# Cross-attention on one core: another order of GpSimd's last instructions, one sum moved to VectorE, and a mixing product placed ahead of four transposes

## The reference

```
text_p  = H_l @ W_text + b_text            # H_l = x: (4, 2048, 512)
audio_p = H_a @ W_audio + b_audio          # H_a: (4, 77, 384)
Q = layer_norm(text_p, g1, beta1);  K = layer_norm(audio_p, g2, beta2);  V = audio_p
alpha = softmax(Q @ K^T / sqrt(512))       # (4, 2048, 77)
out = layer_norm(alpha @ V @ W_out + b_out + H_l, g_out, beta_out)
```

## Time and profile before

| what | value |
|---|---|
| median of three runs | 271.36 us |
| the profiled execution, its own time | 270.91 us |
| span of the profile | 269.2 us |
| granted TensorE clock, mean | 0.994 |
| TensorE matmul, busy | 253.6 us (94%) |
| VectorE, busy | 234.1 us (87%) |
| ScalarE, busy | 207.2 us (77%) |
| GpSimd, busy | 207.4 us (77%) |
| moved by DMA | 43.25 MB |

### The profile page before, as it was taken

The page is one execution under the profiler, slowest core; times in us unless marked ns, Lnnn a source line. Parts: engine busy times, 40 slices in busy tenths (PEclk is TensorE's granted clock), DMA queues, the critical chain, the costliest instruction groups (busy, mean ns, idle before and its releaser), DMA issues.

```text
span 269.2 us, 5946 instructions
## 1 busy us (share of the span) xinstructions
PE 253.6 (94%) x1667; PEld 232.3 (86%) x1667; DVE 234.1 (87%) x719; ACT 207.2 (77%) x516; POOL 207.4 (77%) x232
## 2 busy tenths in 40 slices
PE   7799999999999999999999999999999999999750
PEld 6578878989999989999999999999999999999520
DVE  3867489978999998999999999999999999998594
ACT  3766348235788888989988898888889889999681
POOL 6057440011189999999999999999999999999985
PEclk9999999999999999999999999999999999999997
DMA  6926099532225553544555445444444455442217
GB/s 195 266 80 195 2 280 393 151 131 72 78 80 168 167 175 138 175 160 157 177 181 179 168 169 173 165 156 156 156 158 159 169 169 162 160 171 108 106 46 273
DMA packets 19456, 43.25 MB, mean 161 GB/s; under 512 B 2050, under 2 KB 2382, under 8 KB 19434
## 3 DMA queue, kind: packets, MB, share of 16 engines
q1 hardware_dynamic: 18810, 41.96, 46.6%
q10 hardware_dynamic: 624, 1.06, 1.4%
HBM read 21.19 MB, written 16.78 MB: 141 GB/s over the span
## 4 chain that ended last, share of the span: by engine, by line
PE 73%; POOL 11%; DVE 5%; DMA 5%; ACT 2%; issue 2%; SPq 1%; POOLq 0%; ACTq 0%; DVEq 0%
PE psY L1332 24%; PE psY L1343 11%; PE psT L1261 9%; PE psO L1355 9%; PE psY L1336 4%; DMA zs<-in_ctx_dram 3%; POOL zs L464 3%; POOL zs L458 3%; PE psE L1311 2%; PE psE L1312 2%; DMA xs<-in_x_dram 2%; PE psY L1153 2%; POOL rstd L470 2%; POOL zs L494 1%; POOL zs L498 1%
## 5 line engine op out<-in xcount | busy, mean ns | idle before, releaser
L1332 PE MATMUL psY<-proj,x_hi 128*128 128x336 f32 x512 | 103.1, 323 | 0.0
L1332 PEld LDWEIGHTS psY<-proj,x_hi 128*128 128x128 f32 x512 | 82.7, 189 | 5.6 <-issue 0.4
L464 POOL TENSOR_TENSOR zs<-zs,shift 128x512 f32<-128x512 f32 x54 | 68.6, 1292 | 0.0
L458 POOL TENSOR_TENSOR zs<-zs,gain 128x512 f32<-128x512 f32 x54 | 68.5, 1290 | 0.0
L470 POOL TENSOR_TENSOR rstd<-stat_eps,neg_half 128x4 f32<-128x4 f32 x30 | 30.5, 1017 | 37.8 <-DVE stat_eps L970 35.9
L1343 PE MATMUL psY<-proj,x_lo 128*128 128x336 f32 (+1 forms) x256 | 50.7, 320 | 0.0
L958 DVE CUSTOM_DVE_ANT_0 waste_dve<-psY,xs,sums 128x515 bf16<-128x515 f32 x64 | 48.4, 756 | 2.3
L662 ACT ACTIVATE zs<-hid,shift,rstd 128x512 f32<-128x512 f32 x59 | 47.9, 812 | 0.0
L978 DVE SCALAR_TENSOR_TENSOR hid<-psO,inv_sum,xs 128x512 f32<-128x512 f32 x60 | 44.8, 746 | 2.0 <-PE psO L1355 0.8
L620 ACT ACTIVATE x_hi<-psT 128x512 fp32r<-128x512 f32 x64 | 38.1, 595 | 9.0 <-PE psT L1261 6.9
L856 DVE TENSOR_TENSOR x_lo<-psT,x_hi 128x512 fp32r<-128x512 f32 x64 | 43.6, 681 | 0.6 <-ACT x_hi L620 0.6
(11 more groups left out here) (264 smaller groups left out, 420.2 us busy)
## 6 DMA issues: line engine op xcount, KB each, us to landing
xs<-in_x_dram SPq DMA_DIRECT2D x64, 256.0 KB, 2.9
out_dram<-zs SPq DMA_DIRECT2D x29, 512.0 KB, 2.9
proj<-proj SPq DMA_DIRECT2D x4, 768.0 KB, 9.4
out_dram<-zs SPq DMA_DIRECT2D x6, 256.0 KB, 2.1
xs<-in_L_xattn_W_text_dram SPq DMA_DIRECT2D x4, 256.0 KB, 4.2
xs<-in_L_xattn_W_out_dram SPq DMA_DIRECT2D x2, 512.0 KB, 4.2
wa<-in_L_xattn_W_audio_dram SPq DMA_DIRECT2D x1, 768.0 KB, 6.7
zs<-in_ctx_dram SPq DMA_DIRECT2D x1, 462.0 KB
```

The lines of the kernel that those rows point to most:

```text
L458: nc.gpsimd.tensor_tensor(zs[:, q, t, :], zs[:, q, t, :], gain[:], ALU.mult).then_inc(zg_ready, 1)
L464: nc.gpsimd.tensor_tensor(zs[:, q, t, :], zs[:, q, t, :], shift[:], ALU.add).then_inc(out_ready, 1)
L1332: nc.tensor.matmul(psY[:, t, to:to + HALF], x_hi[:, par, t, k * P:(k + 1) * P], proj[:, q, k, right * HALF:(right + 1) * HALF], start=(k = ...
```

## The change

On TensorE, `fill(0)` issues the mixing product first and the four transposes behind it. On GpSimd, the tail has another order, and the shift of tile 0 of step 29 is taken out of it. VectorE makes that sum in a new `shifted`, as its last instruction, from `SHIFT_P`, the copy of `shift` in PSUM. The last store waits for VectorE instead of GpSimd; its place in the queue is the same.

```
-            store(LAST - 2, 0, out_ready, T * (LAST - 2) + 1)
+            store(LAST - 2, 0, out_tail, 6)
...
             late_gain(LAST - 4, 0)
             late_gain(LAST - 4, 1)
+            inverse_root(STEPS, (LAST + 2) % B, 0, 1)
             late_shift(LAST - 4, 0)
-            late_shift(LAST - 4, 1)
-            inverse_root(STEPS, (LAST + 2) % B, 0, 1)
-            late_gain(LAST - 3, 0)
             inverse_root(STEPS + 1, (LAST + 2) % B, 1, 2 * T - 1)
             mean_shift(STEPS + 1, LAST - 2)
+            late_shift(LAST - 4, 1)
+            late_gain(LAST - 3, 0)
+            inverse_root(STEPS + 2, (LAST - 1) % B, T, T)
+            late_gain(LAST - 3, 1)
             late_shift(LAST - 3, 0)
-            late_gain(LAST - 3, 1)
-            inverse_root(STEPS + 2, (LAST - 1) % B, T, T)
-            late_shift(LAST - 3, 1)
             inverse_root(STEPS + 3, LAST % B, T, 1)
             late_gain(LAST - 2, 0)
             inverse_root(STEPS + 4, LAST % B, T + 1, 1)
-            late_shift(LAST - 2, 0)
+            late_shift(LAST - 3, 1)
...
+            def shifted(j, t):
+                q = j % B
+                dve.wait_ge(zg_ready, T * j + t + 1)
+                nc.vector.tensor_tensor(zs[:, q, t, :], zs[:, q, t, :], SHIFT_P, ALU.add).then_inc(out_tail, 1)
...
             scaled(LAST, 1, STEPS + 4, 5)
+            shifted(LAST - 2, 0)
...
                 def fill(t):
-                    transpose_x(b, i, t)
                     if t == 0 and live(3):
                         mix(b, i, 0, 3)
+                    transpose_x(b, i, t)
```

## The result

| | before | changed |
|---|---|---|
| median of 20 runs each | 270.68 us | 272.14 us |
| ratio, 95% interval | | 1.0079 [1.0054, 1.0104] |
| the profiled execution, time (span) | 270.91 (269.2) us | 272.06 (270.3) us |

By the ratio the change costs 0.8%, or 2.1 us (1.5 to 2.8 us by the interval). Some executions of both kernels fall into a slower state, and the ratio is taken from the others alone; the quotient of the two medians, of all 20 runs each, is 1.0054, or 1.5 us. The forecast was 273.0 us, +2.1 us on the execution profiled.

The account below looks back on a forecast made before the run. The loop was taken as a ring over TensorE and VectorE, the very end as the DMA engines'. 270.91 + 1.0 (loop) + 1.1 (stores) = 273.0 us; 8-in-10 range 270.2 to 275.1.

Parts of the forecast that it names:

- The halves of it: Loop +1.0 us (29 steps of +0.035), bounds -1.2 and +2.3; stores at the end +1.1 us, bounds +0.3 and +1.9.
- the burst of 1.57 MB: End of the kernel: step 28's store waits for GpSimd until 264.50, four stores behind it; all go out together, +1.1 us.
- The rate in the sum: Store burst at the end: 388 GB/s taken from the trace, between 435 for the ports and about 358 for HBM.
- The added sum: VectorE's new last instruction in the tail: takes 0.68 to 0.75 us, ends by 264.8, costs nothing.
- The term of the sum: TensorE's loop: the mixing load waits for parts_t, +0.035 us a step, ends -0.04 and +0.08; 29 steps give +1.0 us.
- the late x: Loop: x waited for once, 0.6 us; rival 2 had it covered by transposes 0.46 us later, worth -0.5 us.
- rival 2: Faster: rival 1's loop, late x covered (-0.5 us), no burst of stores (-1.5 in place of +1.1); 267.7 us, 8%.
- The rule on weight loads: A matmul can begin before its weight load completes; without a gap the loop would cost about -2.2 us; not used.
- Rival 1: TensorE's load finds parts_t ready, loop falls to TensorE's floor: -0.04 a step, -1.2 us, +1.1 at the end; 270.8 us, 20%.
- Rival 3: Slower: the wait for parts_t before the mixing load, up to +0.08 us a step, +2.3; with the stores 274.3 us, 22%.
- the ring over VectorE and ScalarE: Loop, argued for rival 3: both engines shifted by 0.46 us with hundredths to spare, so the ring may lengthen through them.

Follow-up runs that it names:

- The experiment with the stores: Kernel before with only the tail's new order, and step 28 stored tile by tile, ahead of and behind step 31's stores; ratio to before 0.9936, median 268.74 us.
- the tail alone: Changed kernel with `fill` as before, so only the tail and last store differ from the kernel before; ratio to before 1.002, mean step 6.342 us.
- the halves: Changed kernel with ScalarE's copy of the transposed probabilities in two halves, one per tile, each with its own count; ratio to before 0.999, mean step 6.307 us.
- one matmul later: Changed kernel with mixing product and transposes behind three matmuls of the first projection, not two; ratio to before 1.0073, mean step 6.381 us.

## Why the prediction was right

**The sum.** +2.1 us were forecast; the ratio gives 0.0079 x 270.68 = 2.1, and the medians differ by 1.5. The halves of it, +1.0 and +1.1, were +0.9 and +1.3 in the traces. The time itself, 272.06 us, came 0.9 under the 273.0, since the start phase was 1.0 us shorter in this execution. That the two 2.1 meet so closely is in part luck, as the loop shows.

**The tail** came as counted: GpSimd's last shift was forecast to end 17.02 us after the start of the tail's first root (264.50 against 247.48), and ends 17.13 after it (264.48 against 247.35); the burst of 1.57 MB was forecast to end 21.92 us after that same start (269.4 against 247.48), and ends 22.05 after it. The rate in the sum is slightly off: 1.31 MB between 262.6 and 266.05 is 380 GB/s and not 388. The burst itself ran at about 385, 1.57 MB in the 4.1 us from 265.3 to 269.4, so this costs the forecast less than 0.1 us. Of the 0.2 us that the tail lies over the forecast, GpSimd's last shift has 0.11. The added sum took 0.68 us behind VectorE's last result, as the lower of its bounds said, and costs nothing. The experiment with the stores shows that the named cause, the block behind step 28 in the program order of the queue, is the whole of it.

**The loop** has the right mechanism with a mis-sized term and one that was left out. That they cancel is luck. The term of the sum was +0.035 us a step. It holds for the steps whose load carries the wait (6.36 against 6.33). On half of them the wait is an instruction of its own, 0.07 us dearer; the kernel before has that on one step of four only, at its load for the transposes. So inside TensorE's loop the mean is +0.058 (+0.060 over the last 20), and the 22 such steps behind the longest one make +1.3 us. In the steps ahead of that loop the kernel before has the dearer wait on nearly every step (6.37 to 6.41 us), and both orders take the same: +0.1 over all of them.

The term left out is the late x. The sum put the 0.6 us of the earlier trace rows at nothing, without a reason, and gave it to rival 2. All eleven traces have their longest step at this same place: 7.09, 6.58, 7.06 and 7.01 us in the four with the transposes first, 6.47 to 6.69 in the seven with the mixing product first, where the transposes, and so the need for x, come 0.46 us later. Between the two kernels compared that gives back 7.09 - 6.64 = 0.45 us. 1.3 + 0.1 - 0.45 = +0.9. The size of it is not fixed by the order: the tail alone, with the transposes first, has 6.58 there, less than the changed kernel. That it is x that is late is in all eleven traces: one load of x takes 4.4 to 5.1 us to land at this place, and the first transpose starts 0.12 us after the landing (0.15 in one trace). In the kernel before, of the five loads from 86 to 100 us:

```profile
DMA to landing us min/median/max: 2.5/2.8/4.9
```

It is issued at 95.4 us and lands at 100.26, and the transpose starts at 100.38. Why this one load takes so long stays open. The DMA engines were not full in its last part: they moved 4 GB/s from 98 to 99 us and 18 from 99 to 100.

**The rule on weight loads.** The forecast weighed the Trainium skill, "TensorE: Matmul & The Clock Gate", section "Architectural detail: the array is 16x 32x32, not 1x 128x128", as if it meant no gap. The trace after has the load at 182.15 for 0.19 us, and the second matmul at 182.48, so with 0.23 for a matmul the first began at 182.25. The trace's own row has it begin at 182.18 already, as that of the earlier trace rows has 260.24. By either figure it did begin before its load had ended, as the page says. But the second matmul comes 0.33 us behind the start of the load, 0.10 more than the 0.23 of one matmul, and this is what counts behind a wait.

**The rivals.** Rival 1, the floor of TensorE, did not come by itself, but the halves reached it: 6.307 us, -0.04 a step as its bound said. Rival 3 named the place of the dearer wait, not its cause; the ring over VectorE and ScalarE, which it feared, has room for ScalarE's second copy, but not for a product one matmul later, where it costs 0.07 us a step. Rival 2 assumed that the burst does not form; with the stores moved it does not, and the tail then gains 1.1 us.

## What to carry to other kernels

When the last results of an engine are made earlier, read the queue of stores in its program order and ask which store now waits longest: everything behind it waits too, and a store split by tile can be moved to where its data are. When two pieces of work change places in an engine's stream, compare what each waits for and when that arrives; putting the one first whose input arrives at the same moment gains nothing, and here an input that could be had 0.2 us earlier decided whether the new order is a loss or a gain. If a wait binds, see that the instruction that needs it carries it (0.07 us a step here).

## What the runs showed of the hardware

- A wait as an instruction of its own ahead of a weight load: the load starts 0.11 to 0.12 us after the copy that it waits for; carried by the load, 0.05 us. Moving it from two steps of four to three moved the long steps with it (6.405 to 6.416 us). In the kernel before, TensorE's load behind VectorE's x_lo shows the same two distances, 0.12 and 0.05 us.
- In a burst the stores leave SyncE's queue at uneven distances: 0.38, 0.47, 0.83 and 0.68 us between the five stores at the end of the changed kernel (264.51, 264.89, 265.36, 266.19 and 266.87 us), the last two after the DMA engines had filled at 265.3; the tail alone has 0.38, 0.47, 0.84 and 0.68. That the full engines are the cause is not shown. It costs nothing there, since the engines have work until 269.4.
- One load of x takes 4.4 to 5.1 us to land, at the same step in all eleven traces; its neighbours in the kernel before take 2.5 to 3.5.
